# A vision tower with a recurrence and experts on one core: small matmuls moved behind the second layer, and the gates' turn behind the sums' turn

## The reference, cut to what matters

```python
h = patches(x) @ W.T + b                              # 16 steps, 784 tokens, 64 channels
xp = layernorm(h) @ W_ih.T + b_ih + b_hh              # recurrence over the 16 steps
hidden[t] = tanh(xp[t] + hidden[t - 1] @ W_hh.T)
h = h + hidden
x = layernorm(h)                                      # 16 experts, each token takes its best 2
topk_vals, topk_idx = top_k(x @ gate_w + gate_b, 2)
y = relu(einsum('bsh,ehf->bsef', x, w1) + b1)         # first layer, 64 -> 128
expert_out = einsum('bsef,efh->bseh', y, w2) + b2     # second layer, 128 -> 64
moe = sum(softmax(topk_vals) * chosen expert_out)
out = h + (layernorm(x + moe) * gamma + beta)
```

## Time and profile before

| | |
|---|---|
| median of 3 runs | 517.15 us (516.72 to 517.75) |
| the profiled execution | 517.41 us |
| its span, first to last instruction | 515.3 us |
| PE busy | 493.1 us, 96% |
| PEld busy | 324.0 us, 63% |
| DVE busy | 447.4 us, 87% |
| ACT busy | 342.9 us, 67% |
| POOL busy | 184.6 us, 36% |
| mean granted TensorE clock | 0.981 |

### The profile page before, as it was taken

How to read it: one execution, slowest core, us unless ns; L and a number is a source line. 1 busy time by engine, 2 the same in 40 slices (tenths; PEclk the granted TensorE clock), 3 DMA queues, 4 the chain that set the end, 5 groups by cost and what they waited for, 6 DMA issues and landing times.

```text
span 515.3 us, 8772 instructions
## 1 busy us (share of the span) xinstructions
PE 493.1 (96%) x2976; PEld 324.0 (63%) x2976; DVE 447.4 (87%) x881; ACT 342.9 (67%) x586; POOL 184.6 (36%) x137
## 2 busy tenths in 40 slices
PE   7498999999999999999999999999999999999993
PEld 5375666666666666666666666666666666665652
DVE  1567797999989899999989899898989999999775
ACT  1446575858668586766858585776858676665652
POOL 3202213615244352615244361524436252223133
PEclk9869999999999999999999999999999999999997
DMA  6208476674819394483909476482929457481911
GB/s 135 82 5 195 112 174 136 148 179 115 192 44 225 83 198 124 114 198 95 224 27 202 119 173 154 105 200 68 222 61 194 113 125 166 111 199 44 221 47 31
DMA packets 31067, 69.04 MB, mean 134 GB/s; under 512 B 6720, under 2 KB 10800, under 8 KB 30896
## 3 DMA queue, kind: packets, MB, share of 16 engines
q1 hardware_dynamic: 31024, 68.49, 57.6%
HBM read 60.39 MB, written 8.08 MB: 133 GB/s over the span
## 4 chain that ended last, share of the span: by engine, by line
PE 90%; DVE 2%; DMA 2%; issue 2%; POOL 1%; SPq 1%; ACT 1%; POOLq 0%; DVEq 0%
PE pZ L911 38%; PE pO L928 35%; PE pA L830 3%; PE pA L863 2%; PE pA L853 2%; PE pA L880 2%; PE pA L942 2%; PE pB L892 1%; PE pA L843 1%; PE pB L942 1%; PE pB L880 1%; PE pO L802 1%; PE pA L854 1%; DMA spread<-gates_dram 1%; POOL inv_std L366 1%
## 5 line engine op out<-in xcount | busy, mean ns | idle before, releaser
L503 ACT ACTIVATE hexp<-pZ,b1c 128x784 f32<-128x784 f32 x256 | 221.5, 912 | 108.4 <-PE pZ L911 108.4
L928 PE MATMUL pO<-hexp,w2s 128*64 128x392 f32 x1024 | 198.5, 503 | 0.6 <-DVE prod L679 0.3
L911 PE MATMUL pZ<-xt,w1hi 128*128 128x392 f32 x512 | 187.8, 367 | 0.6 <-ACT xt L431 0.6
L679 DVE SCALAR_TENSOR_TENSOR prod<-pO,b2c,spread 128x392 f32<-128x392 f32 x256 | 149.8, 620 | 32.0 <-PE pO L928 28.4
L911 PE MATMUL pZ<-xt,w1lo 128*128 128x392 f32 x512 | 173.8, 339 | 0.0
L911 PEld LDWEIGHTS pZ<-xt,w1hi 128*128 128x128 f32 x512 | 96.1, 188 | 46.1 <-issue 18.3
L366 POOL TENSOR_TENSOR inv_std<-var,nhalf 112x7 f32<-112x7 f32 x48 | 82.2, 1719 | 109.5 <-DVE var L569 109.5
L928 PEld LDWEIGHTS pO<-hexp,w2s 128*64 128x64 f32 x1024 | 70.2, 136 | 75.3 <-issue 62.2
L695 DVE TENSOR_TENSOR acc<-acc,prod 128x784 f32<-128x784 f32 x111 | 113.1, 1019 | 0.1
L911 PEld LDWEIGHTS pZ<-xt,w1lo 128*128 128x128 f32 x512 | 96.4, 188 | 0.0
L379 POOL TENSOR_TENSOR h2b<-h2c,bet 112x448 f32<-112x448 f32 x15 | 18.5, 1231 | 160.1 <-DMA h2c<-h_dram 160.1
(11 more groups left out here) (114 smaller groups left out, 501.3 us busy)
## 6 DMA issues: line engine op xcount, KB each, us to landing
spread<-gates_dram SPq DMA_DIRECT2D x126, 392.0 KB, 9.0
h_dram<-h SPq DMA_DIRECT2D x16, 248.1 KB, 2.4
h2c<-h_dram SPq DMA_DIRECT2D x16, 248.1 KB, 8.8
out<-yo SPq DMA_DIRECT2D x15, 196.0 KB, 8.9
xcur<-x_in SPq DMA_DIRECT2D x16, 112.0 KB, 7.7
xcur<-x_in SPq DMA_DIRECT2D x16, 84.0 KB, 8.5
w1f<-w SPq DMA_DIRECT2D x2, 512.0 KB, 5.9
spread<-gates_dram SPq DMA_DIRECT2D x4, 196.0 KB, 4.0
```

The lines of the kernel that those rows point to most:

```text
L503: nc.scalar.activation(hexp[u % RING][:, :].rearrange("p (b c) -> p b c", b=2), halves(pZ[u % 2]), ACT.Relu, bias=b1c[:, u:u + 1]).then_in ...
L679: nc.vector.scalar_tensor_tensor(out=prod[q % RING][:, b * HALF:(b + 1) * HALF], in0=halves(pO)[:, b, :], scalar=b2c[:, q:q + 1], in1=spre ...
L911: last = nc.tensor.matmul(halves(pZ[e % 2])[:, b, :], w[:, e, :], xt[par][:, b * HALF:(b + 1) * HALF], start=(k == 0), stop=(k == 1))
L928: last = nc.tensor.matmul(halves(pO)[k * D:(k + 1) * D, b, :], w2s[:, e, :], hexp[e % RING][:, b * HALF:(b + 1) * HALF], start=True, stop= ...
```

## The change

On TensorE, `embed_turn`, `recur` and `gates_turn` stood between the first layers and the second layer of their group; now the second layer comes first. `gates_turn` also goes from u = 11 (13 in the first body) to u = 13, behind the second layer there, and so behind `sum_turn`, which stays at u = 11. The waits follow the new order: `sum_turn` no longer waits for `gt` but for what wrote or read pA and pB before it, and `gates_turn` waits until VectorE has read the turned sums (`center`). On ScalarE the copy of the turned xn goes from behind relu 3 to behind relu 4, the tanh from behind relu 5 to behind relu 6, the copy to `gt` from behind relu 11 (13 in the first body) to behind relu 14, and the copy to `xt` in the first body from behind relu 7 to behind relu 8. The order of VectorE, GpSimd and SyncE and all instructions themselves stay as they are.

```diff
--- before.py
+++ after.py
@@ -507,17 +507,17 @@
                 for u in range(E):
                     if experts and not (known(t, 1) and u < 2):
                         relu(t, u)
-                    if gate and u == at(t, 1, first=7):
+                    if gate and u == at(t, 1, first=8):
                         keep_xt(t + 1, 1 - par)
                     if embed and u == at(t, 9, first=11):
                         keep_h1(t + 3, 1 - par)
-                    if mix and u == 3:
+                    if mix and u == 4:
                         keep_xn1t(t + 2)
-                    if mix and u == 5:
+                    if mix and u == 6:
                         new_hidden(t + 2)
                     if gate and u == at(t, 6, first=8):
                         exp_gap(t + 1)
-                    if gate and u == at(t, 11, first=13):
+                    if gate and u == 14:
                         keep_gt(t + 1)
                     if mix and u == at(t, 9, first=11):
                         square_h2(t + 2)
@@ -882,8 +882,10 @@
                                                    ident[0:P, 0:P])
                     last.then_inc(MIX.sem, 1)
 
-            def gates_turn(s, embed):
+            def gates_turn(s, embed, close=False):
                 GATE.wait(pe, s, "gates")
+                if close:
+                    CLOSE.wait(pe, s - 2, "center")
                 if embed and not known(s, 1):
                     pe.wait_ge(h1_kept, 2 * (s + 2) + 2)
                 elif known(s, 1):
@@ -929,10 +931,12 @@
                                                 hexp[e % RING][:, b * HALF:(b + 1) * HALF], start=True, stop=True)
                     last.then_inc(y_ready, 1)
 
-            def sum_turn(s, par, gate=False, mix=False):
+            def sum_turn(s, par, gate=False, mix=False, embed=False):
                 pe.wait_ge(summed, s * Q + Q)
-                if gate:
-                    GATE.wait(pe, s + 2, "gt")
+                if embed:
+                    pe.wait_ge(h1_kept, 2 * (s + 4) + 2)
+                elif gate:
+                    MIX.wait(pe, s + 2, "xt_b")
                 if mix:
                     STATE.wait(pe, s + 3, "h2")
                 if not known(s, 1):
@@ -961,25 +965,25 @@
                 for u in range(E):
                     if experts and not (known(t, 1) and u < 2):
                         first_layer(t, u, par)
+                    if experts and u % 2 == 1:
+                        if u > 1:
+                            second_layer(t, u // 2 - 1)
+                        elif not known(t, 1):
+                            second_layer(t - 1, Q - 1)
                     if mix and u == 3:
                         embed_turn(t + 2)
                     if mix and u == 5:
                         recur(t + 2)
                     if gate and known(t, 1) and u == 7:
                         x2_turn(t + 1)
-                    if gate and u == at(t, 11, first=13):
-                        gates_turn(t + 1, embed)
-                    if experts and u % 2 == 1:
-                        if u > 1:
-                            second_layer(t, u // 2 - 1)
-                        elif not known(t, 1):
-                            second_layer(t - 1, Q - 1)
                     if mix and u == at(t, 7, first=9):
                         hidden_turn(t + 2)
                     if embed and u == at(t, 9, first=11):
                         embed_in(t + 3)
                     if close and u == 11:
-                        sum_turn(t - 1, 1 - par, gate, mix)
+                        sum_turn(t - 1, 1 - par, gate, mix, embed)
+                    if gate and u == 13:
+                        gates_turn(t + 1, embed, close)
                     if gate and not known(t, 1) and u == 1:
                         x2_turn(t + 1)
 
```

## The result

The changed kernel takes **524.99 us** (median of 5 runs, 522.77 to 526.22), the kernel before beside it 517.15 us (5 runs, 515.68 to 517.75). The ratio is 1.0155, with a 95% interval of 1.0128 to 1.0183: slower by 1.6%. The profiled execution took 522.77 us, with a span of 520.7 us; that of before was 517.4 us with 515.3 us, so the span grew by 5.4 us. The forecast was 522.9 us, 5.7 us more than before by its own sum; the medians lie 7.8 us apart.

The account below looks back on a forecast made before the run. TensorE, busy 300.00 of 300 us, sets the pace. 0.9 + 2.0 + 3.0 + 0.9 - 1.1 = +5.7 us takes the profiled 517.4 to 523.1; the median is 0.26 lower: 522.9 us, range 516.2 to 533.

Parts of the forecast that it names:

- The chain: Gates' way from the copy to `gt` through write and spread to second layer 1: starts 6.4 us later against the experts.
- T: Start of first layer 14 on TensorE, from which the times are counted; 270.23 us in the rows of the kernel before.
- part 0: First part of `spread`, two DMAs: predicted to land 6.25 us after the first spread issue, at T + 11.08.
- The small cover of 0.12 us: At second layer 1 in ordinary steps: it can start at T + 11.76, TensorE wants it at T + 11.88.
- in time everywhere: Rival: the spread just makes it and only the order's gain stays, less the last steps; 516.1 us, chance 0.26.
- 0.9 + 3.0 + 0.9 and 2.0: Predicted waits in us: later reads from step 10 on, instruction fetches, jitter in nine ordinary steps; and the last two steps.
- The order of TensorE: Two turns behind a second layer save 0.04 us each in some 14 steps, recurrence unchanged: 1.1 us off.
- The fetches: Instruction fetches while part 0 is under way: some 4 in 14 steps, 3 found, 3 x 1.0 = 3.0 us.
- GpSimd, costed at nothing: GpSimd's work on `h2c` starts at most some 5 us later; without its cover, 1 to 2 us a step.
- the new wait for `center` is met: At `gates_turn`: work after pair 4's product ends at 269.3, the turn comes at about 269.8, so no wait.
- DVE's own run: By itself VectorE would start the product of pair 0 at T + 11.05, against part 0 landing at T + 11.08.

Follow-up runs that it names:

- Experiments 3: The changed kernel with the copy to `gt` one place earlier, ahead of relu 14 on ScalarE: 515.74 us, ratio 0.9988.
- experiment 4: The changed kernel with the copy to `gt` one place later, behind relu 15 instead of relu 14: 544.95 us, ratio 1.0517.
- experiment 7: The changed kernel with the copy to `gt` ahead of relu 14, and the recurrence, its copy and tanh back in their old places: 515.86 us, ratio 0.9983.
- experiment 8: The changed kernel with the first part of `spread` split in every step, pair 0 on its own semaphore: 517.53 us, ratio 1.0027.
- experiment 5: The kernel before with only the recurrence moved behind second layer 1 and its tanh behind relu 6: 520.49 us, ratio 1.0082.
- experiments 1 to 9: Nine follow-up kernels: parts of the change alone, the copy to `gt` earlier or later, and repairs; measured from 513.95 to 544.95 us.

## Why the prediction came out right, point by point

**The chain.** Each link was where it was put: issue at T + 2.36 (2.42), spread issue at T + 4.76 (4.83), landing T + 11.21 (11.08), second layer 1 wanted at T + 11.87 (11.88). The gates' issue to the first spread issue took 2.39 to 2.42 us in all 15 steps. The Trainium skill, "DMA: Bandwidth & Descriptors", section "Anatomy of one DMA — SWDGE (gpsimd) path", fits about 2.0 us and the bytes over 436 GB/s to DMAs that GpSimd issues, while here SyncE issues them; an estimate by it has part 0 landing 2.4 us sooner, in time. The measured landings, 8.7 to 9.0 us behind the gates' issue where no fetch is near, don't bear that out. Experiments 3 and 4 tie the loss to this chain: a relu earlier takes all of it away, a relu later adds 20 us. The small cover of 0.12 us turned into 0.18 us of wait: the landing is 0.18 later, and from it to second layer 1 are 0.79 us (0.02 to the product, 0.77 from there) where I had 0.68. TensorE comes 0.01 sooner. The rival "in time everywhere" had named T + 11.2 for the landing as its point of decision; it fell there by hundredths. That the ordinary steps wait at all was luck as much as reckoning.

**The sum.** Waits: 3.67 us in the steps and 1.93 + 1.20 in the last two, 6.8 us; predicted were 0.9 + 3.0 + 0.9 and 2.0, also 6.8. The split was not right: the steps had less, the last two more (3.1 against 2.0). The order of TensorE was predicted at -1.1 us and gave 13 x -0.02, -0.3 us: the two turns gave 0.03 and 0.07 us a step (four transposes take 0.37 and 0.33 us behind a second layer), but the recurrence there costs 0.08 more than between the layers (1.40 + 0.89 = 2.29 us against 0.62 + 1.59 = 2.21, where nothing waits).

Five further terms were not foreseen. Three are told below: -2.0 us at the head, +1.6 us of clock, and +0.6 us where the turn of the gates waits. The other two bring the sum down. A second layer 1 that had to wait leads to the recurrence in 1.34 us instead of 1.40 (281.42 to 282.76 above; 1.40 at 133.06, the one step that didn't wait): 12 x 0.06, -0.7 us. And the tail of the kernel before had losses of its own that are gone, 0.3 us in front of this line and 0.3 us in smaller ones: -0.6 us.

```profile
461.21 1.54 PE L928 MATMUL pO<-hexp,w2s 128*64 128x392 f32 x8 [0.26 <-ACT hexp L503]
```

6.8 - 0.3 - 2.0 + 1.6 + 0.6 - 0.7 - 0.6 is 5.4, the 5.4 measured between the two profiled executions. So the forecast of 5.7 was met there by errors of opposite sign. Against the medians, 7.8 us apart, it was 2.1 us low, and what the slower executions spent more isn't in any trace here.

**The fetches.** The number, some four, and their sum held, 2.7 us against 3.0, but not the price of each, which ran from nothing to 1.4 us; and the reason given for their place didn't hold. The prediction said that they move out of the gates' window against the chain. In fact in steps 4, 8, 10 and 14 one comes 2.1 to 2.6 us behind the gates' issue, too late for the write (gap 2.41) and in time for the reads. The place alone doesn't decide it: in experiment 7 one at 2.5 us goes with a gap of 4.5 us. Step 10, SP's issues, landing, and what followed:

```profile
331.43 1.23 SPq L283 DMA_DIRECT2D gates_dram<-gt  x2
333.84 5.53 SPq L295 DMA_DIRECT2D spread<-gates_dram  x8
```

```profile
DMA to landing us min/median/max: 4.8/5.7/6.7
```

```profile
341.26 1.16 DVE L679 SCALAR_TENSOR_TENSOR prod<-pO,b2c,spread 128x392 f32<-128x392 f32 x2 [1.15 <-DMA spread<-gates_dram]
...
342.03 1.54 PE L930 MATMUL pO<-hexp,w2s 128*64 128x392 f32 x8 [1.00 <-DVE prod L679]
```

Landing some 9.8 us behind the gates' issue, against 8.8: 0.9 us, and TensorE waits 1.0. In step 4 a fetch cost 0.4 us, in step 8 nothing, in step 14 some 1.4.

**GpSimd, costed at nothing**, was not quite nothing. `h2c` comes later, as said, but the prediction looked only at who needs the result. In the step at 290 us (POOL, DVE, TensorE in the timeline):

```profile
293.23 1.07 POOL L379 TENSOR_TENSOR h2b<-h2c,bet 112x448 f32<-112x448 f32 x1 [14.80 <-DMA h2c<-h_dram]
...
295.29 1.32 POOL L372 TENSOR_TENSOR h<-h,tokb 112x567 f32<-112x567 f32 x1
295.47 1.97 DVE L695 TENSOR_TENSOR acc<-acc,prod 128x784 f32<-128x784 f32 x1
...
298.50 0.54 DVE L602 TENSOR_REDUCE cen<-pB 112x192 f32<-112x384 f32 x1
...
299.14 0.54 PE L894 MATMUL pB<-ident,gates 112*32 112x112 f32 x4 [0.45 <-issue]
```

GpSimd's add had begun 0.18 us before DVE's and had 1.14 us left. DVE's add takes 1.97 us instead of the 0.96 that it takes otherwise. `center` is done late (299.04), and the turn of the gates, which the change makes wait for it, starts 0.45 us late. It happened twice here, 0.6 us in all, and four times in experiment 8, 2.0 us in all. That "the new wait for `center` is met" held for the other steps.

The kernel before has such long adds too, so it is their place that the change moves. What decides is which of the two begins first. Of the kernel before, first GpSimd ahead of DVE, then DVE ahead:

```profile
116.43 1.31 POOL L372 TENSOR_TENSOR h<-h,tokb 112x567 f32<-112x567 f32 x1 [1.59 <-ACT h L423]
116.65 1.92 DVE L695 TENSOR_TENSOR acc<-acc,prod 128x784 f32<-128x784 f32 x1
...
140.70 0.96 DVE L695 TENSOR_TENSOR acc<-acc,prod 128x784 f32<-128x784 f32 x1
140.71 1.90 POOL L379 TENSOR_TENSOR h2b<-h2c,bet 112x448 f32<-112x448 f32 x1 [9.68 <-DMA h2c<-h_dram]
```

In the first pair GpSimd's add had 1.08 us left, and DVE's took 0.83 us more than that. In the second DVE keeps its 0.96 us, and GpSimd's add takes 1.90 us instead of 1.08.

**The clock.** Not foreseen. Behind the 1.93 us wait in step 14:

```profile
459.00:461.00 2.00, 0.09 (x1) 0.01 (x1) 0.75 (x2) 1.14 (x2) 0.00 (x0) 1.00 1.01 216
461.00:463.00 2.00, 1.98 (x6) 0.85 (x8) 1.93 (x5) 0.00 (x0) 0.00 (x0) 0.50 1.05 223
463.00:465.00 2.00, 2.00 (x9) 1.17 (x6) 1.93 (x7) 0.00 (x0) 0.00 (x0) 0.64 1.05 223
465.00:467.00 2.00, 2.00 (x13) 0.94 (x11) 0.99 (x2) 1.81 (x3) 0.00 (x0) 1.00 1.03 223
```

The columns are the window, its length, the busy time of PE, PEld, DVE, ACT and POOL, the granted clock, the DMA share and GB/s. TensorE does next to nothing from 459 to 461, then the granted clock is 0.50 and 0.64: half speed, 1.2 of 2.4 GHz, for 3.4 us of these windows. The second layer took 2.81 us to the next first layer instead of 1.47, and that one 0.3 us more: +1.6 us. So this wait cost nearly twice its length; the 1.20 us wait in the last step was followed by no fall.

**The head.** Not foreseen, and a gain. In the first body `embed_turn` and `x2_turn` used to stand ahead of a second layer and waited 1.09 us each for DVE with TensorE idle. Behind it, only one of them still waits:

```profile
41.75 0.60 PE L843 MATMUL pA<-ident,xn 112*128 112x112 f32 x4
...
49.63 0.60 PE L880 MATMUL pA<-ident,x2hl 112*128 112x112 f32 x4 [0.32 <-DVE x2hl L607]
```

With the turn of xn in its old place, in experiment 5, the first wait is back:

```profile
40.66 0.60 PE L843 MATMUL pA<-ident,xn 112*128 112x112 f32 x4 [1.09 <-DVE xn L580]
```

**What the prediction had as a number and never used as a limit** is DVE's own run to its product of pair 0, T + 11.05, 0.2 us ahead of the landing. In most steps of the whole change it doesn't show, because the gates part moves T by 0.35 us against that run. In two, 9 and 11, both behind a long add of DVE, the product comes without idle time after the landing, and TensorE waits about 0.2 us for DVE's run and not for `spread`. Undoing the gates part on the strength of the prediction gave 519.3 us where 516.6 was expected.

## What to carry to other kernels

Before an operation is moved, write down for its new place every limit with its time (the transfer, the other engine's own run, the copy), not only the latest one: here three stood within 0.2 us of each other, and each part of the change uncovered another. A gain of some hundredths per turn isn't worth starting a fixed chain of copy, write, receipt and broadcast 6 us later; if the order is wanted, start the chain a relu earlier and split its first transfer so that the first reader waits for its own half alone. And a small wait on an engine that is busy at all times isn't the whole price: fetches and the clock come on top where it gets long.

## What the hardware showed that was not expected

- One 16 KB packet of the instruction queue goes with a delay of the transfers beside it, which differs from case to case. Where it came 1.6 to 2.0 us behind the issue of the gates' write (49 KB), the gap to the dependent issue was 3.9 to 4.3 us instead of 2.4 (kernel before, experiments 4 and 7); on the reads of 2 x 392 KB in the changed kernel the landing was up to 1.4 us later, and in step 8 not later at all. The Trainium skill, "Runtime: NRT & Kernel Launch", on the mechanics of instruction fetch, calls the cost of such a block to the fetching engine's own program mostly hidden; what it does to other transfers the page doesn't say, and here it is hidden only while they have time in hand.
- TensorE's granted clock fell to half behind waits of 1.93 us (changed kernel) and 2.40, 3.20 and 2.13 us (experiment 4), and not behind waits of 2.44 and 2.37 us in the same experiment. The length of the wait alone doesn't decide it; what does, no run here shows.
- DVE's add of 128 x 784 elements, 0.96 us by itself, took 0.83 us plus what was left of GpSimd's add when that one had begun earlier. This holds within 0.01 us for all 138 such adds in the traces of before, after and experiments 1 to 9 (GpSimd at least 0.1 us ahead, with over 0.15 us left). Begun first, DVE's add kept its 0.96 us and GpSimd's took the delay.
